# A fused attention and int8 feed-forward kernel: where the sums of the probabilities grow, and how wide they are when the ones product takes them

## The chip, the cores and the metric

The kernel runs on one core of a Trainium2 chip. TensorE (PE) multiplies matrices and writes to PSUM, VectorE (DVE) and ScalarE (ACT) work element by element, GpSimd (POOL) does a little at the ends, and SyncE (SP) issues most transfers. The metric is the device time of one execution in microseconds: 1489.73 us before, the median of three runs (1487.76 to 1489.96). Each engine takes its instructions in the written order; between engines the order comes from waits on semaphores.

## The reference

Cross attention of 1024 queries against 2048 context rows, for 2 batch entries and 16 heads of 64, then a feed-forward product in int8. What matters here is the attention:

```python
q = (lat @ Wq); k, v = split(ctx @ Wkv); k = apply_rope(k, cos, sin)
attn = einsum('bhnd,bhsd->bhns', q, k) * 64 ** -0.5
attn = clip(attn, -11.0, 11.0)
attn = softmax(attn, axis=-1)
out  = einsum('bhns,bhsd->bhnd', attn, v) @ Wo + bo
x    = x + tanh(g_xattn) * out
# then: layer norm, rows scaled to int8, times an int8 matrix, gated and added
```

The softmax needs, for each query and head, the sum of 2048 exponentials. The kernel clips after the exponential (CLIP_LOW is e^-11, CLIP_HIGH is e^11), adds the clipped values on VectorE as far as the rows go on different partitions, and sums over the 128 partitions with a matrix of ones on TensorE.

## The kernel before

It has three stages: projections (up to about 475 us of the span), attention (to about 1369 us), and the output stage. The change lies in attention, `attention` from L760 on, and in `PairEnds`, which turns sums into reciprocals.

Attention goes over 16 *pairs* of heads (n). A pair has 32 *units*: for each of two *halves* of 512 queries, 16 steps of 128 context rows. A unit's scores for both heads are 1024 columns in one of three PSUM banks. Four units are a *batch*, so a pair has 8 batches b, numbered 0 to 7; batches 0 to 3 are the first half and 4 to 7 the second. In all there are 32 halves.

The engines share the work so:
- TensorE, for each batch: the scores of batch b (`scores`, 24 matmuls), then the values of batch b-1 (`values`, the product of probabilities and v, accumulated in `value_ps` over a half). Once per half, in batches 1 and 5, it multiplies the sums with ones into `sum_ps` (`sums`, L914): four products, one for each of two heads and of two sums, each into its own 32 partitions.
- ScalarE: the exponentials of each unit into `prob` (L966). `prob` has two places of 4096 columns, taken in turn. It also copies `value_ps` and `sum_ps` to SBUF once per half (L973, L979).
- VectorE, for each batch: the clip in place, 4096 columns (`clip`, L1050), then the additions (`add_probs`). Batch 0 or 4 adds its two halves of 2048 columns into `prob_sum` (L1062); the other three batches each add their two halves to it, one after the other (L1066). In batches 1 and 5 `normalise` (L206) multiplies the output of the half before by its reciprocal sums; in batches 3 and 7 `reciprocals` adds the two reloaded sums of 8 columns (L192) and inverts them (L197).
- SyncE: the sums to DRAM and back in another layout, reciprocals likewise, output, and the k, q and v of the pair after next.

The order on each engine is written out by hand (the `pair` function of each), for the most part inside a loop that runs over two pairs at a time. What holds the parts together around the change: a clip waits for its four exponentials (`exped`), values wait for the clip (`clipped`), an addition waits for the one before (`added`), ones wait for all additions of the half, and an exponential waits until the place in `prob` that it writes has been multiplied (`valued`) and added.

Of the kernel before, what the change touches and what calls it, by code (L numbers as in the profile page):

```python
# [12 lines left out]
P = 128  # L13
# [26 lines left out]
def flamingo_kernel(  # L40
# [20 lines left out]
    sum_scr = nc.dram_tensor("sum_scr", (ALLPAIRS, 2, 4, CH), F32, kind="Internal").ap()  # L61
# [60 lines left out]
class Late:  # L122

    def __init__(self, sb, sem, o_raw, o_out):
# [10 lines left out]
        self.sum_row = sb("sum_row", [P, CH])  # L135
        self.sum_sq = sb("sum_sq", [P, 2, 4, CH // P])
        self.sum_both = sb("sum_both", [P, 2, 2, CH // P])
# [6 lines left out]
        self.sum_joined = sem("sum_joined")  # L144
# [7 lines left out]
class PairEnds:  # L152
# [9 lines left out]
    def load_sums(self, sp, n, half):  # L162
        late = self.late
        sp.wait_ge(late.sum_stored, 16 * (2 * n + half + 1))
        sp.dma_start(late.sum_sq[:, half, :, :], self.sum_scr[n, half].rearrange("g (p j) -> p g j", p=P)
                     ).then_inc(late.sum_in[half], 16)
# [21 lines left out]
    def reciprocals(self, dve, n, half):  # L188
        late = self.late
        turn = 2 * n + half  # L190
        dve.wait_ge(late.sum_in[half], 16 * (n + 1))
        dve.tensor_tensor(late.sum_both[:, half, :, :], late.sum_sq[:, half, 0:2, :], late.sum_sq[:, half, 2:4, :],  # L192
                          ALU.add).then_inc(late.sum_joined, 1)
        dve.wait_ge(late.sum_joined, turn + 1)
        if not isinstance(n, int) or n >= 1:
            dve.wait_ge(late.rec_stored[half], 16 * n)
        dve.reciprocal(late.rec_sq[:, half, :, :], late.sum_both[:, half, :, :]).then_inc(late.rec_made, 1)  # L197
# [557 lines left out]
def attention(nc, ctx, load_pair, k_st, q_st, v_st, kqv_in, v_stored, late, ends, gate_tanh, wo, bo, rhs_t,  # L755
# [8 lines left out]
    ADDS = 2 * HALF_BATCHES - 1  # L764
# [4 lines left out]
    prob_sum = sb("prob_sum", [P, 2, 2, 2, CH])  # L769
# [33 lines left out]
    def first(n, k=1):  # L803

        return isinstance(n, int) and n < k

# [67 lines left out]
    def _(pe):  # L874
# [17 lines left out]
        def values(n, slot, b):  # L892
# [3 lines left out]
            for i in range(BATCH_UNITS):  # L896
                s = (b * BATCH_UNITS + i) % STEPS
                for a in range(2):
                    rows = slice(a * DHEAD, (a + 1) * DHEAD)
                    last = pe.matmul(value_ps[rows, :], v_st[slot][:, s, rows], prob[:, b % 2, i, a * CH:(a + 1) * CH],  # L900
                                     start=(s == 0), stop=(s == STEPS - 1))
            last.then_inc(valued, 1)

        def sums(n, half):
# [6 lines left out]
            for j in range(2):  # L911
                for a in range(2):
                    row = (2 * j + a) * SUM_ROWS
                    last = pe.matmul(sum_ps[row:row + SUM_ROWS, :], ones[:, 0:SUM_ROWS], prob_sum[:, half, j, a, :],  # L914
                                     start=True, stop=True)
# [42 lines left out]
    def _(act):  # L958
        def exps(n, b):
            for u in range(b * BATCH_UNITS, (b + 1) * BATCH_UNITS):  # L960
                if u % BATCH_UNITS == 0 and not (first(n) and b < 2):

                    act.wait_ge(valued, BATCHES * n + b - 1)
                    act.wait_ge(added, ADDS * (2 * n + (b - 2) // HALF_BATCHES) + 2 * ((b - 2) % HALF_BATCHES) + 1)
                act.wait_ge(scored, UNITS * n + u + 1)
                act.activation(prob[:, b % 2, u % BATCH_UNITS, :], score_ps[:, u % BANKS, :, :], ACT.Exp, scale=SCALE  # L966
# [8 lines left out]
        def copy_sums(n, half):  # L975
# [3 lines left out]
            act.activation(late.sum_row[:, :], sum_ps[:, :], ACT.Copy).then_inc(late.sum_copied, 1)  # L979
# [39 lines left out]
    def _(dve):  # L1019
# [27 lines left out]
        def clip(n, b):  # L1047
            tile = prob[:, b % 2, :, :]
# [3 lines left out]
        def add_probs(n, b):  # L1052

            half, part = divmod(b, HALF_BATCHES)
            total = prob_sum[:, half, :, :, :].rearrange("p j a c -> p j (a c)")
            halves = [prob[:, b % 2, j:j + 2, :] for j in (0, 2)]
            before = ADDS * (2 * n + half) + 2 * part - 1
            dve.wait_ge(clipped, BATCHES * n + b + 1)
            if part == 0:
                if not first(n):  # L1060
                    dve.wait_ge(summed, 2 * (n - 1) + half + 1)
                dve.tensor_tensor(total, halves[0], halves[1], ALU.add).then_inc(added, 1)  # L1062
                return
            for j in range(2):
                dve.wait_ge(added, before + j)
                dve.tensor_tensor(total, total, halves[j], ALU.add).then_inc(added, 1)  # L1066
# [355 lines left out]
```

## Time and profile before

| | |
|---|---|
| device time, median of 3 runs | 1489.73 us |
| device time of the profiled execution | 1489.53 us |
| its span | 1487.7 us |
| TensorE busy, share of the span | 98% |
| VectorE busy, share of the span | 84% |
| ScalarE busy, share of the span | 47% |
| values (L900), 2048 records | 468.6 us |
| scores (L888), 3072 records | 396.7 us |
| exponentials (L966), 512 | 483.1 us |
| additions of 2048 columns (L1066 and L1062), 192 and 32 | 446.3 and 75.8 us |
| clips (L1050), 128 | 292.7 us |
| ones products (L914), 256 records | 34.1 us |

An engine's share is an average over three stages, so it can't be read as the load of attention. A float32 matmul leaves two records. The recorded time of one matmul (0.59 us for 512 columns) includes its way through the array, and neighbours overlap, so what a group costs is read from the start of the group to the start of the next. In the idle column, an arrow names what ended the wait.

### The profile page before, as it was taken

The numbers are of one execution on the slowest core, as the hardware profiler recorded it, in microseconds if no ns is written. First come the engines' busy times: TensorE is split into PE (matmuls) and PEld (weight loads), VectorE is DVE, ScalarE is ACT, GpSimd is POOL, SyncE is SP. The second block draws the span as 40 slices with busy tenths as digits, with TensorE's granted clock in tenths as the row PEclk, the third lists the DMA queues.
The fourth block names the chain that finished last, engine by engine and source line by source line (L and its number), as shares of the span: only waits on it lengthen the run. The fifth ranks groups of instructions, "written<-read, shape, count | busy, mean of one in ns | idle before, by whom it ended". The sixth has DMA issues, their size and how long they took to land. (4 is left out here: it accounts for less than half of the span.)

```text
span 1487.7 us, 22575 instructions
## 1 busy us (share of the span) xinstructions
PE 1458.5 (98%) x8090; PEld 886.2 (60%) x8090; DVE 1246.0 (84%) x1108; ACT 706.5 (47%) x823; POOL 118.7 (8%) x71
## 2 busy tenths in 40 slices
PE   8999999999999899999999999999999999999997
PEld 7888888888887344444444444444444444444774
DVE  6756666667655999999999999999999999997997
ACT  4432222222223556565655656565656556564332
POOL 0500000000000300000000000000000000001775
PEclk9999999999999999999999999999999999999998
DMA  7783655555667623523532532541551551402652
GB/s 269 249 260 135 205 170 170 186 157 165 193 172 253 165 48 96 129 60 98 133 70 81 135 92 58 135 101 48 135 127 27 130 134 37 121 16 72 171 169 85
DMA packets 144496, 195.60 MB, mean 131 GB/s; under 512 B 36160, under 2 KB 85312, under 8 KB 138304
## 3 DMA queue, kind: packets, MB, share of 16 engines
q1 hardware_dynamic: 141296, 189.71, 45.3%
q10 hardware_dynamic: 3152, 5.25, 0.9%
q8 instruction: 30, 0.49, 0.1%
q14 instruction: 18, 0.15, 0.0%
HBM read 114.83 MB, written 80.08 MB: 131 GB/s over the span
## 5 line engine op out<-in xcount | busy, mean ns | idle before, releaser
L966 ACT ACTIVATE prob<-score_ps 128x1024 f32<-128x1024 f32 x512 | 483.1, 1032 | 187.1 <-PE score_ps L888 184.3
L900 PE MATMUL value_ps<-prob,v_st 128*64 128x512 f32 x2048 | 468.6, 599 | 4.9 <-DVE prob L1050 4.9
L1066 DVE TENSOR_TENSOR prob_sum<-prob_sum,prob 128x2048 f32<-128x2048 f32 x192 | 446.3, 2325 | 13.6 <-DVE prob L1050 0.2
L888 PE MATMUL score_ps<-q_st,k_st 64*128 64x512 f32 x3072 | 396.7, 403 | 7.9 <-ACT prob L966 5.8
L888 PEld LDWEIGHTS score_ps<-q_st,k_st 64*128 64x128 f32 x3072 | 272.8, 186 | 177.5 <-issue 103.1
L1050 DVE TENSOR_SCALAR prob<-prob 128x4096 f32<-128x4096 f32 x128 | 292.7, 2287 | 41.0 <-ACT prob L966 38.8
L900 PEld LDWEIGHTS value_ps<-prob,v_st 128*64 128x64 f32 x2048 | 135.8, 137 | 272.9 <-issue 265.0
L644 DVE TENSOR_TENSOR k_cos<-k_raw,rope 128x1024 f32<-128x1024 f32 x32 | 39.2, 1225 | 100.0 <-ACT k_raw L548 100.0
L553 ACT ACTIVATE v_out<-proj_ps 128x1024 f32<-128x1024 f32 x31 | 31.9, 1028 | 136.7 <-PE proj_ps L230 136.7
L548 ACT ACTIVATE k_raw<-proj_ps 128x1024 f32<-128x1024 f32 x31 | 31.9, 1029 | 105.1 <-PE proj_ps L230 105.1
L1062 DVE TENSOR_TENSOR prob_sum<-prob 128x2048 f32<-128x2048 f32 x32 | 75.8, 2368 | 1.8 <-DVE prob L1050 0.2
L1386 POOL MEMSET unround<- 128x1 f32 x1 | 0.1, 98 | 844.1 <-POOLq L116 844.1
L230 PE MATMUL proj_ps<-tok_hi,wkv_hi 128*128 128x512 f32 x248 | 67.0, 392 | 0.0
L230 PE MATMUL proj_ps<-tok_hi,wkv_lo 128*128 128x512 f32 x248 | 66.3, 389 | 0.0
L230 PE MATMUL proj_ps<-wkv_lo,tok_hi 128*128 128x512 f32 x248 | 66.3, 389 | 0.0
L230 PE MATMUL proj_ps<-wkv_hi,tok_hi 128*128 128x512 f32 x248 | 66.3, 389 | 0.0
L230 PE MATMUL proj_ps<-wkv_hi,tok_lo 128*128 128x512 f32 x248 | 66.3, 389 | 0.0
L230 PE MATMUL proj_ps<-tok_lo,wkv_hi 128*128 128x512 f32 x248 | 66.3, 389 | 0.0
L979 ACT ACTIVATE sum_row<-sum_ps 128x512 f32<-128x512 f32 x32 | 19.2, 599 | 93.4 <-PE sum_ps L914 93.4
L230 PEld LDWEIGHTS proj_ps<-tok_hi,wkv_lo 128*128 128x128 f32 x248 | 46.6, 188 | 9.8
L230 PEld LDWEIGHTS proj_ps<-wkv_hi,tok_hi 128*128 128x128 f32 x248 | 46.6, 188 | 9.7
L230 PEld LDWEIGHTS proj_ps<-tok_lo,wkv_hi 128*128 128x128 f32 x248 | 46.6, 188 | 9.7
(123 smaller groups left out, 1333.6 us busy)
## 6 DMA issues: line engine op xcount, KB each, us to landing
k_st<-k_scr SPq DMA_DIRECT2D x128, 256.0 KB, 6.5
k_scr<-k_hi SPq DMA_DIRECT2D x64, 256.0 KB, 2.7
v_scr<-v_out SPq DMA_DIRECT2D x32, 512.0 KB, 3.4
k_scr<-k_lo SPq DMA_DIRECT2D x64, 256.0 KB, 4.0
q_st<-q_scr SPq DMA_DIRECT2D x16, 1024.0 KB, 10.9
v_st<-v_scr SPq DMA_DIRECT2D x16, 1024.0 KB, 13.8
q_scr<-q_hi SPq DMA_DIRECT2D x32, 256.0 KB, 4.3
q_scr<-q_lo SPq DMA_DIRECT2D x32, 256.0 KB, 4.4
```

What stands on the lines that cost most here:

```text
L230: last = pe.matmul(acc, s, m, start=(n == 0), stop=(n == len(terms) - 1))
L548: act.activation(k_raw[:, j % 2, :, :], banks(what, j, order), ACT.Copy).then_inc(k_copied, 1)
L553: act.activation(v_out[:, j, :], banks(what, j, order), ACT.Copy).then_inc(v_copied, 1)
L644: last = dve.tensor_tensor(made[:, :, :], k_raw[:, s, :, :], rope[:, slot, f:f + 1, :].broadcast_to((P, 2, CH)), ALU.mult)
L888: last = pe.matmul(score_ps[:, u % BANKS, a, :], k_st[slot][rows, k_part, s * P:(s + 1) * P], q_st[slot][rows, q_part, cols], start=(t == ...
L900: last = pe.matmul(value_ps[rows, :], v_st[slot][:, s, rows], prob[:, b % 2, i, a * CH:(a + 1) * CH], start=(s == 0), stop=(s == STEPS - 1))
L966: act.activation(prob[:, b % 2, u % BATCH_UNITS, :], score_ps[:, u % BANKS, :, :], ACT.Exp, scale=SCALE).then_inc(exped, 1)
L979: act.activation(late.sum_row[:, :], sum_ps[:, :], ACT.Copy).then_inc(late.sum_copied, 1)
L1050: dve.tensor_scalar(tile, tile, CLIP_LOW, CLIP_HIGH, ALU.max, ALU.min).then_inc(clipped, 1)
L1062: dve.tensor_tensor(total, halves[0], halves[1], ALU.add).then_inc(added, 1)
L1066: dve.tensor_tensor(total, total, halves[j], ALU.add).then_inc(added, 1)
L1386: pool.memset(unround[:, :], -ROUND).then_inc(unround_set, 1)
```

## The change

It does five things.
- The first batch of a half is no longer added. Its exponentials are written straight into `prob_sum`, which is now as wide as a batch (4096 columns, one for each half). It is clipped there, and TensorE takes its values from there (`home`). The other three batches use the two places of `prob`, six batches of a pair in turn (`tenant` works out who had the place before).
- The other three batches are added in one instruction of 4096 columns each. The first of the three writes over batch 0 or 4, and so waits for `valued` of that batch.
- Behind the last addition of the half, two more fold the sum: 4096 columns into 2048, then 2048 into 1024 (one unit's width). There are 5 additions per half in place of 7 (`ADDS`).
- The ones product has four products of 256 columns in place of four of 512; the copy of `sum_ps` and the sums in DRAM are half as large.
- `reciprocals` has no addition any more: one inversion of the reloaded sums.

VectorE at the end of one half and the start of the next, in the loop: the end of batch 3, then batch 4 and the start of batch 5. L1050 is the clip, L192 the joining addition of 8 columns, L197 the reciprocal, L1062 and L1066 the additions of 2048 columns; the rest is waits and register work. Before:

```order
L192 TENSOR_TENSOR sum_both<-sum_sq 128x8 [waits sum_in1]
L194 REGISTER_ALU
L197 RECIPROCAL rec_sq<-sum_both 128x8 [waits rec_stored1,sum_joined]
L1049 REGISTER_ALU
L1050 TENSOR_SCALAR prob<-prob 128x4096 [waits exped]
L1058 REGISTER_ALU
L1062 TENSOR_TENSOR prob_sum<-prob 128x2048 [waits summed,clipped]
L1049 REGISTER_ALU
L1050 TENSOR_SCALAR prob<-prob 128x4096 [waits exped]
L1058 REGISTER_ALU
L1065 ISA [waits clipped]
L1066 TENSOR_TENSOR prob_sum<-prob_sum,prob 128x2048 [waits added]
```

In the code before, an addition of 2048 columns stands between the clip of batch 4 and that of batch 5, and the addition of batch 5 waits for VectorE's own work only. The same place after, from the first fold on; L1081 and L1083 are the folds, L191 the reciprocal, L1064 the clip, L1078 the wide addition:

```order
L1081 TENSOR_TENSOR prob_sum<-prob_sum 128x2048 [waits added]
L1082 REGISTER_ALU
L1083 TENSOR_TENSOR prob_sum<-prob_sum 128x1024 [waits added]
L191 RECIPROCAL rec_sq<-sum_sq 128x8 [waits rec_stored1,sum_in1]
L1063 REGISTER_ALU
L1064 TENSOR_SCALAR prob_sum<-prob_sum 128x4096 [waits exped]
L1063 REGISTER_ALU
L1064 TENSOR_SCALAR prob<-prob 128x4096 [waits exped]
L1073 REGISTER_ALU
L1075 REGISTER_ALU [waits clipped]
L1078 TENSOR_TENSOR prob_sum<-prob_sum,prob 128x4096 [waits valued]
```

The two folds have come ahead of the clip of batch 4 (the one on `prob_sum`), the addition between the two clips is gone, and the addition of batch 5 stands behind a wait on `valued`.

TensorE around the ones product in batch 1 of the second pair (the last two units' scores, the values of batch 0, the ones product, the next scores), before:

```order
L888 MATMUL score_ps<-q_st,k_st 128x512 [waits exped]
L888 MATMUL score_ps<-q_st,k_st 128x512 x5
L900 MATMUL value_ps<-prob,v_st 64x512 [waits o_copied,clipped]
L900 MATMUL value_ps<-prob,v_st 64x512 x7
L914 MATMUL sum_ps<-prob_sum,ones 32x512 [waits sum_copied,added]
L914 MATMUL sum_ps<-prob_sum,ones 32x512 x3
L888 MATMUL score_ps<-q_st,k_st 128x512 [waits exped]
L888 MATMUL score_ps<-q_st,k_st 128x512 x5
```

The ones product (L914) there has 512 columns for each of its four matmuls. And after:

```order
L896 MATMUL score_ps<-q_st,k_st 128x512 [waits exped]
L896 MATMUL score_ps<-q_st,k_st 128x512 x5
L908 MATMUL value_ps<-prob_sum,v_st 64x512 [waits o_copied,clipped]
L908 MATMUL value_ps<-prob_sum,v_st 64x512 x7
L923 MATMUL sum_ps<-prob_sum,ones 32x256 [waits sum_copied,added]
L923 MATMUL sum_ps<-prob_sum,ones 32x256 x3
L896 MATMUL score_ps<-q_st,k_st 128x512 [waits exped]
L896 MATMUL score_ps<-q_st,k_st 128x512 x5
```

The order is the same; the values of the half's first batch now come from `prob_sum`, and the ones product is half as wide.

```diff
--- before.py
+++ after.py
@@ -58,7 +58,7 @@
 
     k_scr = nc.dram_tensor("k_scr", (BATCH, QUADS, 4, P, NS), F32, kind="Internal").ap()
     v_scr = nc.dram_tensor("v_scr", (BATCH * NS, INNER), F32, kind="Internal").ap()
-    sum_scr = nc.dram_tensor("sum_scr", (ALLPAIRS, 2, 4, CH), F32, kind="Internal").ap()
+    sum_scr = nc.dram_tensor("sum_scr", (ALLPAIRS, 2, 4, CH // 2), F32, kind="Internal").ap()
     rec_scr = nc.dram_tensor("rec_scr", (ALLPAIRS, 2, 2, CH), F32, kind="Internal").ap()
 
     o_scr = nc.dram_tensor("o_scr", (BATCH, INNER, NQ), F32, kind="Internal").ap()
@@ -132,16 +132,14 @@
         self.o_raw = o_raw
         self.o_out = o_out
         self.recip = sb("recip", [P, NQ])
-        self.sum_row = sb("sum_row", [P, CH])
-        self.sum_sq = sb("sum_sq", [P, 2, 4, CH // P])
-        self.sum_both = sb("sum_both", [P, 2, 2, CH // P])
+        self.sum_row = sb("sum_row", [P, CH // 2])
+        self.sum_sq = sb("sum_sq", [P, 2, 2, CH // P])
         self.rec_sq = sb("rec_sq", [P, 2, 2, CH // P])
         self.o_loaded = [sem(f"o_loaded{i}") for i in range(2)]
         self.o_hi_made = sem("o_hi_made3")
         self.sum_copied = sem("sum_copied")
         self.sum_stored = sem("sum_stored")
         self.sum_in = [sem(f"sum_in{i}") for i in range(2)]
-        self.sum_joined = sem("sum_joined")
         self.rec_made = sem("rec_made")
         self.rec_stored = [sem(f"rec_stored{i}") for i in range(2)]
         self.rec_in = [sem(f"rec_in{i}") for i in range(2)]
@@ -162,7 +160,7 @@
     def load_sums(self, sp, n, half):
         late = self.late
         sp.wait_ge(late.sum_stored, 16 * (2 * n + half + 1))
-        sp.dma_start(late.sum_sq[:, half, :, :], self.sum_scr[n, half].rearrange("g (p j) -> p g j", p=P)
+        sp.dma_start(late.sum_sq[:, half, :, :], self.sum_scr[n, half].rearrange("(a h) c -> a (h c)", a=2).rearrange("a (p j) -> p a j", p=P)
                      ).then_inc(late.sum_in[half], 16)
 
     def store_reciprocals(self, sp, n, half):
@@ -187,14 +185,10 @@
 
     def reciprocals(self, dve, n, half):
         late = self.late
-        turn = 2 * n + half
         dve.wait_ge(late.sum_in[half], 16 * (n + 1))
-        dve.tensor_tensor(late.sum_both[:, half, :, :], late.sum_sq[:, half, 0:2, :], late.sum_sq[:, half, 2:4, :],
-                          ALU.add).then_inc(late.sum_joined, 1)
-        dve.wait_ge(late.sum_joined, turn + 1)
         if not isinstance(n, int) or n >= 1:
             dve.wait_ge(late.rec_stored[half], 16 * n)
-        dve.reciprocal(late.rec_sq[:, half, :, :], late.sum_both[:, half, :, :]).then_inc(late.rec_made, 1)
+        dve.reciprocal(late.rec_sq[:, half, :, :], late.sum_sq[:, half, :, :]).then_inc(late.rec_made, 1)
 
     def normalise(self, eng, n, half):
         late = self.late
@@ -761,12 +755,12 @@
     BATCHES = UNITS // BATCH_UNITS
     HALF_BATCHES = BATCHES // 2
     BANKS = 3
-    ADDS = 2 * HALF_BATCHES - 1
+    ADDS = HALF_BATCHES + 1
     k_st.append(sb("k_st1", [P, 2, NS], F32R))
     q_st.append(sb("q_st1", [P, 2, NQ], F32R))
     v_st.append(sb("v_st1", [P, STEPS, P]))
     prob = sb("prob", [P, 2, BATCH_UNITS, 2 * CH])
-    prob_sum = sb("prob_sum", [P, 2, 2, 2, CH])
+    prob_sum = sb("prob_sum", [P, 2, BATCH_UNITS, 2 * CH])
     wo_raw = sb("wo_raw", [P, 2, DIM])
 
     rhs_amax = sb("rhs_amax", [P, KT])
@@ -803,6 +797,20 @@
     def first(n, k=1):
 
         return isinstance(n, int) and n < k
+
+    def home(b):
+
+        half, part = divmod(b, HALF_BATCHES)
+        if part == 0:
+            return prob_sum[:, half, :, :]
+        return prob[:, (half * (HALF_BATCHES - 1) + part - 1) % 2, :, :]
+
+    def tenant(b):
+
+        half, part = divmod(b, HALF_BATCHES)
+        seat = half * (HALF_BATCHES - 1) + part - 1 - 2
+        half, part = divmod(seat % (2 * (HALF_BATCHES - 1)), HALF_BATCHES - 1)
+        return (-1 if seat < 0 else 0), half, part + 1
 
     def all_pairs(eng, body):
 
@@ -897,7 +905,7 @@
                 s = (b * BATCH_UNITS + i) % STEPS
                 for a in range(2):
                     rows = slice(a * DHEAD, (a + 1) * DHEAD)
-                    last = pe.matmul(value_ps[rows, :], v_st[slot][:, s, rows], prob[:, b % 2, i, a * CH:(a + 1) * CH],
+                    last = pe.matmul(value_ps[rows, :], v_st[slot][:, s, rows], home(b)[:, i, a * CH:(a + 1) * CH],
                                      start=(s == 0), stop=(s == STEPS - 1))
             last.then_inc(valued, 1)
 
@@ -908,11 +916,12 @@
                 pe.wait_ge(late.sum_copied, 2 * n + half)
             if first(n, 2) and not first(n) and half == 0:
                 pe.wait_ge(row_copied, 1)
-            for j in range(2):
-                for a in range(2):
-                    row = (2 * j + a) * SUM_ROWS
-                    last = pe.matmul(sum_ps[row:row + SUM_ROWS, :], ones[:, 0:SUM_ROWS], prob_sum[:, half, j, a, :],
-                                     start=True, stop=True)
+            for a in range(2):
+                for part in range(2):
+                    row = (2 * a + part) * SUM_ROWS
+                    col = a * CH + part * CH // 2
+                    last = pe.matmul(sum_ps[row:row + SUM_ROWS, 0:CH // 2], ones[:, 0:SUM_ROWS],
+                                     prob_sum[:, half, 0, col:col + CH // 2], start=True, stop=True)
             last.then_inc(summed, 1)
 
         def turn_rhs(part):
@@ -958,12 +967,17 @@
     def _(act):
         def exps(n, b):
             for u in range(b * BATCH_UNITS, (b + 1) * BATCH_UNITS):
-                if u % BATCH_UNITS == 0 and not (first(n) and b < 2):
-
-                    act.wait_ge(valued, BATCHES * n + b - 1)
-                    act.wait_ge(added, ADDS * (2 * n + (b - 2) // HALF_BATCHES) + 2 * ((b - 2) % HALF_BATCHES) + 1)
+                if u % BATCH_UNITS == 0:
+                    if b % HALF_BATCHES == 0:
+                        if not first(n):
+                            act.wait_ge(summed, 2 * n - 1 + b // HALF_BATCHES)
+                    else:
+                        before, half, part = tenant(b)
+                        if not first(n, -before):
+                            act.wait_ge(valued, BATCHES * (n + before) + half * HALF_BATCHES + part + 1)
+                            act.wait_ge(added, ADDS * (2 * (n + before) + half) + part)
                 act.wait_ge(scored, UNITS * n + u + 1)
-                act.activation(prob[:, b % 2, u % BATCH_UNITS, :], score_ps[:, u % BANKS, :, :], ACT.Exp, scale=SCALE
+                act.activation(home(b)[:, u % BATCH_UNITS, :], score_ps[:, u % BANKS, :, :], ACT.Exp, scale=SCALE
                                ).then_inc(exped, 1)
 
         def copy_values(n, half):
@@ -976,7 +990,7 @@
             act.wait_ge(summed, 2 * n + half + 1)
             if not (first(n) and half == 0):
                 act.wait_ge(late.sum_stored, 16 * (2 * n + half))
-            act.activation(late.sum_row[:, :], sum_ps[:, :], ACT.Copy).then_inc(late.sum_copied, 1)
+            act.activation(late.sum_row[:, :], sum_ps[:, 0:CH // 2], ACT.Copy).then_inc(late.sum_copied, 1)
 
         def copy_rhs(part):
             act.wait_ge(rhs_turned, part + 1)
@@ -1045,25 +1059,28 @@
                 made.then_inc(rhs_step, 1)
 
         def clip(n, b):
-            tile = prob[:, b % 2, :, :]
+            tile = home(b)
             dve.wait_ge(exped, UNITS * n + (b + 1) * BATCH_UNITS)
             dve.tensor_scalar(tile, tile, CLIP_LOW, CLIP_HIGH, ALU.max, ALU.min).then_inc(clipped, 1)
 
         def add_probs(n, b):
 
             half, part = divmod(b, HALF_BATCHES)
-            total = prob_sum[:, half, :, :, :].rearrange("p j a c -> p j (a c)")
-            halves = [prob[:, b % 2, j:j + 2, :] for j in (0, 2)]
-            before = ADDS * (2 * n + half) + 2 * part - 1
+            if part == 0:
+                return
+            total = prob_sum[:, half, :, :]
+            before = ADDS * (2 * n + half) + part - 1
             dve.wait_ge(clipped, BATCHES * n + b + 1)
-            if part == 0:
-                if not first(n):
-                    dve.wait_ge(summed, 2 * (n - 1) + half + 1)
-                dve.tensor_tensor(total, halves[0], halves[1], ALU.add).then_inc(added, 1)
-                return
-            for j in range(2):
-                dve.wait_ge(added, before + j)
-                dve.tensor_tensor(total, total, halves[j], ALU.add).then_inc(added, 1)
+            if part == 1:
+                dve.wait_ge(valued, BATCHES * n + b)
+            else:
+                dve.wait_ge(added, before)
+            dve.tensor_tensor(total, total, home(b), ALU.add).then_inc(added, 1)
+            if part == HALF_BATCHES - 1:
+                dve.wait_ge(added, before + 1)
+                dve.tensor_tensor(total[:, 0:2, :], total[:, 0:2, :], total[:, 2:4, :], ALU.add).then_inc(added, 1)
+                dve.wait_ge(added, before + 2)
+                dve.tensor_tensor(total[:, 0, :], total[:, 0, :], total[:, 1, :], ALU.add).then_inc(added, 1)
 
         def pair(n, slot):
             for b in range(BATCHES):
```

## Rows read from the trace of the kernel before

**Rows 1.** the page's first part, busy time of each engine

```profile
PE 1458.5 (98%) x8090; PEld 886.2 (60%) x8090; DVE 1246.0 (84%) x1108; ACT 706.5 (47%) x823; POOL 118.7 (8%) x71
```

**Rows 2.** busy time by stretch: PE, PEld, DVE, ACT, POOL, granted clock, DMA share, GB/s

```profile
500.00:520.00 20.00, 14.99 (x82) 6.77 (x80) 19.80 (x12) 9.93 (x11) 7.27 (x2) 0.91 0.28 88
540.00:560.00 20.00, 17.47 (x106) 7.53 (x104) 19.79 (x15) 10.49 (x12) 0.00 (x0) 1.00 0.51 109
620.00:680.00 60.00, 60.00 (x370) 28.01 (x369) 56.98 (x32) 35.27 (x40) 0.00 (x0) 1.00 0.43 107
```

**Rows 3.** timeline of TensorE, one half: start us, us, instruction

```profile
637.36 1.06 PE L914 MATMUL sum_ps<-prob_sum,ones 128*32 128x512 f32 x8
638.36 3.05 PE L888 MATMUL score_ps<-q_st,k_st 64*128 64x512 f32 x24
641.34 3.65 PE L900 MATMUL value_ps<-prob,v_st 128*64 128x512 f32 x16
...
661.03 3.65 PE L900 MATMUL value_ps<-prob,v_st 128*64 128x512 f32 x16
664.61 1.07 PE L914 MATMUL sum_ps<-prob_sum,ones 128*32 128x512 f32 x8
```

**Rows 4.** timeline of VectorE, the same half

```profile
635.61 2.29 DVE L1050 TENSOR_SCALAR prob<-prob 128x4096 f32<-128x4096 f32 x1 [0.88 <-ACT prob L966]
638.04 4.62 DVE L1066 TENSOR_TENSOR prob_sum<-prob_sum,prob 128x2048 f32<-128x2048 f32 x2
642.58 0.68 DVE L206 TENSOR_TENSOR o_out<-o_raw,recip 128x512 f32<-128x512 f32 x1
643.18 2.29 DVE L1050 TENSOR_SCALAR prob<-prob 128x4096 f32<-128x4096 f32 x1
645.59 4.62 DVE L1066 TENSOR_TENSOR prob_sum<-prob_sum,prob 128x2048 f32<-128x2048 f32 x2
...
657.26 0.20 DVE L197 RECIPROCAL rec_sq<-sum_both 128x8 f32<-128x8 f32 x1
657.38 2.29 DVE L1050 TENSOR_SCALAR prob<-prob 128x4096 f32<-128x4096 f32 x1
659.71 2.29 DVE L1062 TENSOR_TENSOR prob_sum<-prob 128x2048 f32<-128x2048 f32 x1
```

**Rows 5.** VectorE additions: groups by line; one line's min/median/max ns

```profile
L644 DVE TENSOR_TENSOR k_cos<-k_raw,rope 128x1024 f32<-128x1024 f32 x32 | 39.2, 1225 | 100.0 <-ACT k_raw L548 100.0
L1066 DVE TENSOR_TENSOR prob_sum<-prob_sum,prob x192: 2291/2292/4380, 488.0 to 1365.2; 128x2048 f32<-128x2048 f32 x192
```

**Rows 6.** timeline of TensorE in the first two pairs and at the end

```profile
517.50 4.50 PE L900 MATMUL value_ps<-prob,v_st 128*64 128x512 f32 x16
521.94 1.06 PE L914 MATMUL sum_ps<-prob_sum,ones 128*32 128x512 f32 x8
...
549.28 3.66 PE L900 MATMUL value_ps<-prob,v_st 128*64 128x512 f32 x16 [1.40 <-DVE prob L1050]
552.87 1.07 PE L914 MATMUL sum_ps<-prob_sum,ones 128*32 128x512 f32 x8
...
582.65 1.07 PE L914 MATMUL sum_ps<-prob_sum,ones 128*32 128x512 f32 x8
...
1347.81 1.06 PE L914 MATMUL sum_ps<-prob_sum,ones 128*32 128x512 f32 x8
...
1367.55 1.07 PE L914 MATMUL sum_ps<-prob_sum,ones 128*32 128x512 f32 x8 [1.00 <-DVE prob_sum L1066]
```

**Rows 7.** timeline of VectorE in the first pair

```profile
523.26 6.71 DVE L1066 TENSOR_TENSOR prob_sum<-prob_sum,prob 128x2048 f32<-128x2048 f32 x2
...
545.98 1.05 DVE L1044 TENSOR_SCALAR rhs_int<-rhs_raw 128x512 bf16<-128x512 f32 x3
546.94 2.29 DVE L1050 TENSOR_SCALAR prob<-prob 128x4096 f32<-128x4096 f32 x1
```

**Rows 8.** groups by line, VectorE's clip

```profile
L1050 DVE TENSOR_SCALAR prob<-prob 128x4096 f32<-128x4096 f32 x128 | 292.7, 2287 | 41.0 <-ACT prob L966 38.8 <-issue 1.6
```

## The prediction

> **What bounds the kernel now.** I read the page's shares first. TensorE is busy 98% of the span, VectorE 84%, ScalarE 47% [rows 1]. The 84% is an average over stages, so next I read a steady stretch of attention: from 620 to 680 us TensorE is busy 60.00 of 60, at full granted clock, and VectorE 56.98 [rows 2]. VectorE has 5% of slack there, and the change gives it work.
>
> The third view is the timeline of one half: four batches (5, 6, 7 of one pair, then 0 of the next) and the ones product. From one ones product to the next are 27.25 us (637.36 to 664.61) without an idle gap [rows 3]: TensorE sets the pace. Per batch it runs scores (2.98 us) and then the values of the batch *before* (3.58 us), so a batch costs 6.56 us. The ones product adds 1.00 us.
>
> VectorE in the same half [rows 4] has one gap that the data causes: 0.88 us before the clip of batch 5, waiting for ScalarE's exponentials. From that clip to the clip of batch 0 it runs without a break. That clip ends at 659.67, and TensorE wants it at 661.03: 1.4 us of slack. This is the number that the change spends. After the clip of batch 0, VectorE does the half's first addition (2.29 us) while it would wait for the next exponentials anyway, so this addition is free today.
>
> **The change, part by part.** *The free addition goes, and two folds appear.* Batch 0 (and 4) needs no addition. In the half's last batch two folds of 2048 and 1024 columns follow its addition, and the clip of the next batch 0 is queued behind them on VectorE. Work leaves the place where it was hidden and arrives in the place where there were 1.4 us.
>
> *Prices on VectorE.* A 2048-column addition takes 2.292 us, a 1024-column one 1.225 [rows 5]: 1.067 us per 1024 columns. No row has 4096. By the slope it is 2.292 + 2.134 = 4.43 us. The lower end is the slope with no fixed part, 4.27; the upper end is today's pair of additions, 4.62 [rows 4]. I take 4.43. An independent instruction starts 0.08 us before the recorded end of the one ahead (the pair starts at 638.04, lasts 4.62, and the next starts at 642.58), a dependent one 0.04 behind it (4.62 - 2x2.29). So a wide addition holds the engine 4.35 us, or 4.47 if a fold waits for it; the folds 2.33 and 1.23 - 0.08 = 1.15. Per half the additions and folds are 4.35 + 4.35 + 4.47 + 2.33 + 1.15 = 16.65 us, against 3x4.54 + 2.21 = 15.83 today. The joining addition of 8 columns goes, 0.2 us. Net +0.6 us per half: small. What decides is order.
>
> The Trainium skill, "VectorE: DVE Perf Modes", section on the TRN2 errata, holds that the fixed latency is paid once per instruction, so that a single large tile is cheaper, and its rules for kernel authors say to minimise the number of instructions. By that rule alone the change helps: eight instructions become five, about 0.16 us each by the two additions above. The rows agree on the fixed part, but the columns added per half (three times 4096, 2048 and 1024 against seven times 2048) are 1024 more, 1.07 us, so the rule's gain of some 0.5 us is outweighed.
>
> *The new wait.* The addition of batch 1 (5) writes over batch 0 (4), so it waits until TensorE has finished that batch's values. This closes a loop: clip of batch 0, then values of batch 0, then addition of batch 1, then everything of the half on VectorE, then the next clip of batch 0. Queued behind the waiting addition are all later clips, for which TensorE's values wait. VectorE can put only the clip of batch 1 into the 3.65 us of the values.
>
> *The loop, summed,* from the first addition of a half, at A, each from its start to the next start [rows 4]: addition 4.35, normalise 0.60, clip 2.41, addition 4.35, clip 2.41, addition 4.47, folds 2.33 and 1.15, reciprocal 0.12, clip 2.29: 24.48 us. Then values start 0.06 behind the clip (today's stalled example: 546.94 + 2.29 to 549.28 [rows 6, 7]), take 3.65, and the addition starts 0.05 later: 28.24.
> One wait lies inside: the clip of batch 2 (6) needs its exponentials. The ones product starts at A - 0.12, the scores follow, and the clip comes 4.82 us after the scores' start (638.36 to 643.18 [rows 3, 4]).
> The ones product's price: values are eight rounds of two column groups in 3.58 us, today's ones two rounds of four groups in 1.00; so 0.43 per 512-column round and 0.14 fixed. Half the columns give 2x0.215 + 0.14 = 0.57 us (bounds 0.50 and 1.00, the latter if the columns did not count). So that clip starts at A - 0.12 + 0.57 + 4.82 = A + 5.27 and not A + 4.95: +0.32.
> **The loop is 28.56 us.** TensorE needs 27.33 - 0.43 = 26.90, so it idles 1.66 us per half, before the values of batch 0 or 4. The 0.43 us saved on the ones product is lost in that idle time.
>
> *What is hidden.* ScalarE copies 512 columns less 256, and the transfer of sums halves: ScalarE is busy 47% [rows 1], and the copy is on no path but at the very end. SyncE's queue keeps its order; VectorE asks for the reloaded sums behind the folds now, 3.5 us later than before, so what is on time today stays on time. ScalarE's new waits (older values, additions, ones products) are over before scores arrive: batch 7's seat is free when batch 5 is added, A + 4.4, and its scores start at A + 7.0.
>
> **The sum over the run.** The ones products mark the halves [rows 3, 6]: today 521.94, 552.87, 582.65, then 28 steady ones to 1347.81 (27.33 each), and the last at 1367.55.
> - Up to 521.94: VectorE loses the first addition (2.2) and 3x0.2 on the wide ones and gains 3.5 of folds, +0.7; but the values of batch 4 at 517.50 wait there for scores and not for the clip. Between 0 and 0.7, I take 0.
> - 521.94 to 552.87 (30.93): the loop without normalise, with the quantising of the weights between (three gaps, 3.04 us in all; 545.98 to 546.94 is one) and one addition stretched by GpSimd's subtraction (6.71 for 4.62) [rows 7]: 24.48 - 0.60 + 3.04 + 2.09 + 3.76 = 32.77. +1.8.
> - 552.87 to 582.65: TensorE has transposes of its own there and stays the slow one: -0.4.
> - 28 steady halves: 28x28.56 - 765.16 = +34.5. Pauses on issue before VectorE's clips, 1.6 us in all [rows 8] and hidden now, join the loop: +1.5.
> - The end: the last ones product needs both folds. From the one before: 0.12 + 5.27 + 2.41 + 4.35 + 2.41 + 4.47 + 2.33 + 1.23 + 0.05 = 22.64 against 19.74; the product and its copy are some 0.6 shorter before the output stage may start. +2.3.
>
> Sum +39.7 us. The profiled execution took 1489.53 us, so 1529.2. The median of the runs shown is 1489.73, 0.2 above it, so I say 1529.
>
> **The rivals.**
> - *VectorE's throughput alone decides; the loop costs nothing.* It speaks for it that VectorE is the fuller engine after the change. The half would be 24.48 - 0.08 + 2.41 + 0.32 = 27.13 us, 0.20 under today: 1483. It decides from the point at which the values of batch 0 end before the clip of batch 1 does. Against it: values take 3.65 us, the clip 2.41, and both start from the same clip.
> - *TensorE stays the bound* and the saving on the ones shows in full: 32x0.43 = 13.8 us, 1476. That needs the clip of batch 0 to end within 1.4 us of where it ends now, and the folds are 3.5.
> - *The clock falls in the new stalls.* From 500 to 520 us TensorE is busy 14.99 of 20, the granted clock is 0.91 over the stretch (so it fell from the 2.4 GHz level to the 1.2 one for a part of it), and a group of values takes 4.50 and not 3.65 [rows 2, 6]. From 540 to 560 it is busy 17.47 of 20, with one stall of 1.40 us, the clock stays 1.00 and the values take 3.66. The new stall, 1.66 in 28.56, is nearer to the second. A fall in each half adds 0.85 us to the loop: +27, 1556.
> - *The wide addition is not 4.43.* At 4.27 the loop is 0.48 shorter and the time 1514; at 4.62 it is 0.57 longer: 1547.
>
> **How the numbers follow.** The loop with its sum: 0.79, its own range 1520 to 1538. The wide addition near an end: 0.07. A fall of the clock, in all or some halves: 0.07. VectorE's throughput alone: 0.04. TensorE the bound: 0.03. The range takes the addition's two ends, 1514 to 1547, and leaves out the gains and a full fall of the clock. A difference under 0.2% (3 us) can't be told from none. Faster than that: the two gaining cases, 0.07. Within: 0.01, where a case would just cancel. Slower: 0.92.
>
> **What would show it.** In the profile after, ones products 28.5 us apart; TensorE idle some 1.6 us before the values of batch 0 and 4, released by VectorE's clip, and VectorE idle some 1.5 us (3.76 - 2.21) around the clip of batch 1 and 5, the larger part before the addition, released by TensorE's values. A wide addition of 4.43 us, a ones product of 0.57. TensorE's share falls from 98% to about 94 or 95. The forecast is wrong if that stall is missing, if the clip of batch 0 is not behind the folds, or if the ones products stand under 27.3 us apart.

## The result, and the profile after

The changed kernel takes 1531.04 us (median of 5, 1530.15 to 1531.95) against 1489.55 (5 runs, 1487.58 to 1489.96): ratio 1.0281, 95% interval 1.0267 to 1.0295. It is slower by 41.5 us; 1529 was forecast. The span of the profiled execution went from 1487.7 to 1528.1, +40.4 us.

The first part of the page of the changed kernel answers to [rows 1]:

```profile
PE 1450.7 (95%) x8090; PEld 888.3 (58%) x8090; DVE 1261.6 (83%) x1012; ACT 700.2 (46%) x823; POOL 121.5 (8%) x71
```

TensorE works 7.8 us less and VectorE 15.6 us more, in a span that is 40 us longer. Neither amount explains the 40 us, so the engines must wait where they did not before. Here is busy time by stretch of the changed kernel (columns as in [rows 2]):

```profile
545.00:555.00 10.00, 6.15 (x28) 2.03 (x30) 6.86 (x8) 1.32 (x3) 0.00 (x0) 0.83 0.64 136
640.00:700.00 60.00, 56.65 (x362) 27.54 (x362) 55.31 (x23) 33.47 (x39) 0.00 (x0) 1.00 0.36 89
1406.00:1416.00 10.00, 9.26 (x33) 7.29 (x30) 0.78 (x2) 3.64 (x5) 6.03 (x4) 0.70 0.63 183
```

In the steady stretch *no* engine is full: TensorE 56.65 of 60, VectorE 55.31. Before, TensorE was at 60.00. When two engines both wait, look for a loop between them. The timeline of TensorE in the changed kernel, one half, answers to [rows 3]:

```profile
640.36 0.64 PE L923 MATMUL sum_ps<-prob_sum,ones 128*32 128x256 f32 x8
640.93 3.05 PE L896 MATMUL score_ps<-q_st,k_st 64*128 64x512 f32 x24
...
660.62 3.04 PE L896 MATMUL score_ps<-q_st,k_st 64*128 64x512 f32 x24
665.34 3.65 PE L908 MATMUL value_ps<-prob_sum,v_st 128*64 128x512 f32 x16 [1.68 <-DVE prob_sum L1064]
668.92 0.64 PE L923 MATMUL sum_ps<-prob_sum,ones 128*32 128x256 f32 x8
```

The ones products stand 28.56 us apart (668.92 - 640.36), and the only gap is 1.68 us before the values of the half's first batch, ended by VectorE's clip. The ones product itself costs 0.57 (640.36 to 640.93), as worked out. The timeline of VectorE in the same half answers to [rows 4]:

```profile
640.47 4.43 DVE L1078 TENSOR_TENSOR prob_sum<-prob_sum,prob 128x4096 f32<-128x4096 f32 x1 [1.29 <-PE value_ps L908]
644.81 0.69 DVE L200 TENSOR_TENSOR o_out<-o_raw,recip 128x512 f32<-128x512 f32 x1
645.74 2.29 DVE L1064 TENSOR_SCALAR prob<-prob 128x4096 f32<-128x4096 f32 x1 [0.23 <-ACT prob L980]
648.17 4.42 DVE L1078 TENSOR_TENSOR prob_sum<-prob_sum,prob 128x4096 f32<-128x4096 f32 x1
...
659.38 2.29 DVE L1081 TENSOR_TENSOR prob_sum<-prob_sum 128x2048 f32<-128x2048 f32 x1
661.71 1.22 DVE L1083 TENSOR_TENSOR prob_sum<-prob_sum 128x1024 f32<-128x1024 f32 x1
662.85 0.19 DVE L191 RECIPROCAL rec_sq<-sum_sq 128x8 f32<-128x8 f32 x1
662.97 2.24 DVE L1064 TENSOR_SCALAR prob_sum<-prob_sum 128x4096 f32<-128x4096 f32 x1
665.43 2.29 DVE L1064 TENSOR_SCALAR prob<-prob 128x4096 f32<-128x4096 f32 x1 [0.23 <-ACT prob L980]
669.04 4.43 DVE L1078 TENSOR_TENSOR prob_sum<-prob_sum,prob 128x4096 f32<-128x4096 f32 x1 [1.31 <-PE value_ps L908]
```

The folds (659.38, 661.71) stand in front of the clip at 662.97, and the values at 665.34 follow its end (665.21) at once. VectorE then waits 1.31 us for these values. That is 1.54 us around this clip with the 0.23 before it (665.43), where some 1.5 were forecast. The 0.23 us before the clip of batch 2 or 6 (645.74), ended by ScalarE's exponentials, looks harmless; experiment e3 shows that it is as much a part of the loop as the 1.31.

Where the 40.4 us lie, by the starts of the ones products in the two traces: up to the first -2.7 (521.94 to 519.29); first to second +3.7; second to third -0.4; the 28 steady halves +34.2 (799.34 less 765.16, 28.55 us each); the last +2.8; the output stage +2.8.

### The profile page after: what moved, and what is told of

Same layout as the page of the kernel before. It is cut to its first block and busy times, and to the rows that moved or that the text cites. A ratio compares the mean times of both kernels' runs of the same rounds, so it can differ in the third digit from the quotient of the medians.

```text
span 1528.1 us, 22339 instructions
## 1 busy us (share of the span) xinstructions
PE 1450.7 (95%) x8090; PEld 888.3 (58%) x8090; DVE 1261.6 (83%) x1012; ACT 700.2 (46%) x823; POOL 121.5 (8%) x71
## 5 line engine op out<-in xcount | busy, mean ns | idle before, releaser
L1078 DVE TENSOR_TENSOR prob_sum<-prob_sum,prob 128x4096 f32<-128x4096 f32 x96 | 424.8, 4425 | 45.0 <-PE value_ps L908 37.9
L980 ACT ACTIVATE prob<-score_ps 128x1024 f32<-128x1024 f32 x384 | 362.2, 1031 | 109.6 <-PE score_ps L896 108.5
L908 PE MATMUL value_ps<-prob,v_st 128*64 128x512 f32 x1536 | 352.6, 601 | 1.4 <-DVE prob L1064 1.4
L1064 DVE TENSOR_SCALAR prob<-prob 128x4096 f32<-128x4096 f32 x96 | 220.4, 2296 | 20.0 <-ACT prob L980 20.0
L908 PEld LDWEIGHTS value_ps<-prob,v_st 128*64 128x64 f32 x1536 | 102.2, 137 | 203.3 <-issue 200.2
L908 PE MATMUL value_ps<-prob_sum,v_st 128*64 128x512 f32 x512 | 118.4, 605 | 49.3 <-DVE prob_sum L1064 49.3
L980 ACT ACTIVATE prob_sum<-score_ps 128x1024 f32<-128x1024 f32 x128 | 120.8, 1032 | 82.4 <-PE score_ps L896 82.4
L908 PEld LDWEIGHTS value_ps<-prob_sum,v_st 128*64 128x64 f32 x512 | 35.1, 138 | 118.2 <-issue 105.7
L1064 DVE TENSOR_SCALAR prob_sum<-prob_sum 128x4096 f32<-128x4096 f32 x32 | 71.8, 2245 | 10.9 <-ACT prob_sum L980 10.9
L1081 DVE TENSOR_TENSOR prob_sum<-prob_sum 128x2048 f32<-128x2048 f32 x32 | 75.4, 2356 | 1.1
```

The lines of the kernel that those rows point to most:

```text
L980: act.activation(home(b)[:, u % BATCH_UNITS, :], score_ps[:, u % BANKS, :, :], ACT.Exp, scale=SCALE).then_inc(exped, 1)
L1064: dve.tensor_scalar(tile, tile, CLIP_LOW, CLIP_HIGH, ALU.max, ALU.min).then_inc(clipped, 1)
L1078: dve.tensor_tensor(total, total, home(b), ALU.add).then_inc(added, 1)
L1081: dve.tensor_tensor(total[:, 0:2, :], total[:, 0:2, :], total[:, 2:4, :], ALU.add).then_inc(added, 1)
```

## The experiments

Each ran beside the kernel before, on the same chip as it (e1 to e4 on one chip, e5 to e7 on another); ratios are to it. Code cuts are shortened, `...` marks what is left out. Line numbers in the rows are of each kernel's own text.

**e1: the folds behind the next clip.** The additions and folds are those of the changed kernel.

```diff
                 clip(n, b)
+                if b == 0 and not first(n):
+                    fold(n - 1, 1)
+                if b == HALF_BATCHES:
+                    fold(n, 0)
                 add_probs(n, b)
+                if b == BATCHES - 1 and isinstance(n, int) and n == ALLPAIRS - 1:
+                    fold(n, 1)
...
```

`fold(n, half)` holds the same two folds, which are gone from `add_probs`.

> The changed kernel with only the place of the two folds changed: they come behind the clip of the next half's first batch. Nothing else moves, the wait on values stays. Theory A (the folds ahead of that clip hold the values, and so close the loop): VectorE's clip of batch 0 or 4 ends some 3.5 us sooner, TensorE has no stall, and the ones products stand 26.90 us apart (27.33 of before less 0.43 for the narrower ones): about 1478 us, with 2 to 3 us lost at the end of attention. Theory B (the wait on values itself is the cost): VectorE still idles before the first addition and the halves stay near 28.2 us, about 1520. Theory C (VectorE's throughput is the bound after the change): 27.1 us per half, about 1484.

Measured: 1478.12 us (5 runs), ratio 0.993 (0.9917 to 0.9944). The ones products stand 26.90 us apart over 28 steady halves. Timeline of VectorE in e1:

```profile
647.17 4.43 DVE L1078 TENSOR_TENSOR prob_sum<-prob_sum,prob 128x4096 f32<-128x4096 f32 x1
651.52 0.20 DVE L191 RECIPROCAL rec_sq<-sum_sq 128x8 f32<-128x8 f32 x1
651.63 2.24 DVE L1064 TENSOR_SCALAR prob_sum<-prob_sum 128x4096 f32<-128x4096 f32 x1
653.79 2.28 DVE L1084 TENSOR_TENSOR prob_sum<-prob_sum 128x2048 f32<-128x2048 f32 x1
656.11 1.23 DVE L1086 TENSOR_TENSOR prob_sum<-prob_sum 128x1024 f32<-128x1024 f32 x1
657.44 2.29 DVE L1064 TENSOR_SCALAR prob<-prob 128x4096 f32<-128x4096 f32 x1
659.86 4.42 DVE L1078 TENSOR_TENSOR prob_sum<-prob_sum,prob 128x4096 f32<-128x4096 f32 x1
```

The same instructions with the same durations; the folds now fill the place in which VectorE would wait for exponentials, and the addition at 659.86, which still waits for the values by its semaphore, does not wait in fact. TensorE has no stall there: it is busy 270.00 us of the 270 from 906 to 1176 us. Moving two instructions is worth 3.5% by the two ratios, some 52 us. Theory A stands; B (the wait itself costs) falls; C (VectorE's throughput) falls, since 26.90 is TensorE's own time. VectorE, busy 264.18 of the same 270, is close behind it, as e7 shows.

**e2: no folds.**

```diff
-    ADDS = HALF_BATCHES + 1
+    ADDS = HALF_BATCHES - 1
...
-            if part == HALF_BATCHES - 1:
-                dve.wait_ge(added, before + 1)
-                dve.tensor_tensor(total[:, 0:2, :], total[:, 0:2, :], total[:, 2:4, :], ALU.add).then_inc(added, 1)
-                dve.wait_ge(added, before + 2)
-                dve.tensor_tensor(total[:, 0, :], total[:, 0, :], total[:, 1, :], ALU.add).then_inc(added, 1)
```

It leaves out three quarters of each sum: the ones product takes the first unit's columns only.

> The changed kernel without the two folds (it leaves out three of the four units of each batch from the sums; the ones product takes the first unit). Wide additions and the wait on values stay. Theory A: 3.5 us less ahead of the clip of batch 0 or 4, loop 25.1 us, under TensorE's 26.90: TensorE is the bound, about 1474 us, and no stall before values. Theory B: the wait on values costs by itself, over 1500. Against e1 it tells what the folds cost as work rather than by their place: nothing by A (but for 3.5 us at the end).

Measured: 1471.65 us (4 runs), ratio 0.9889 (0.9874 to 0.9904); a steady half takes 26.89 us (1330.16 less 577.20, by 28), as in e1 (26.90). So the folds, 3.5 us of VectorE's time per half, cost nothing as work in the steady halves while they lie behind the clip. The two times are 6.5 us apart. Of the 8.1 us between the two traces (1477.4 and 1469.3), 3.6 lie in the last half and 3.0 behind it (see e5), 1.3 ahead of the first ones product.

**e3: no wait on values.** The first addition of a half writes into a small tile of its own, in four instructions of 1024 columns, so it need not wait for the values; it leaves out this addition's part of the sums.

```diff
...
             if part == 1:
-                dve.wait_ge(valued, BATCHES * n + b)
-            else:
-                dve.wait_ge(added, before)
+                for j in range(4):
+                    if j or half or not first(n):
+                        dve.wait_ge(added, before - 3 + j)
+                    dve.tensor_tensor(aside[:, :], total[:, j, :], home(b)[:, j, :], ALU.add).then_inc(added, 1)
+                return
+            if part == 2:
+                dve.wait_ge(valued, BATCHES * n + b - 1)
+            dve.wait_ge(added, before)
             dve.tensor_tensor(total, total, home(b), ALU.add).then_inc(added, 1)
...
```

> The changed kernel with the first addition of each half written aside, in four instructions of 1024 columns into a small tile, so that it need not wait for the values of the batch it would write over (the sums lack batches 0, 1, 4 and 5's addition: the second addition adds to batch 0 alone). The folds stay where they are. Theory A': the wait on values is only one of two ways in which the loop closes; clip of batch 0, values, ones, scores of batch 2, exponentials, clip of batch 2 is as long (19.53 + 0.06 + 3.58 + 0.57 + 4.82 = 28.56 us), so the halves stay at 28.5 and the time within 5 us of 1531. Theory B (the wait on values closes the loop, and without it VectorE's throughput of 27.1 or TensorE decides): 1483 to 1490 us.

Measured: 1534.56 us (4 runs), ratio 1.031 (1.0294 to 1.0326); 28.62 us per half. Timeline of VectorE in e3:

```profile
640.16 2.29 DVE L1065 TENSOR_SCALAR prob<-prob 128x4096 f32<-128x4096 f32 x1 [0.18 <-ACT prob L981]
642.59 5.00 DVE L1079 TENSOR_TENSOR aside<-prob_sum,prob 128x1024 f32<-128x1024 f32 x4
647.51 0.68 DVE L200 TENSOR_TENSOR o_out<-o_raw,recip 128x512 f32<-128x512 f32 x1
649.08 2.29 DVE L1065 TENSOR_SCALAR prob<-prob 128x4096 f32<-128x4096 f32 x1 [0.89 <-ACT prob L981]
```

The wait before the first addition is gone (642.59 follows the clip directly), and the idle time has moved to the clip of batch 2 or 6: 0.89 us, for exponentials whose scores come after the late values. The four narrow additions take 5.00 us and not 4.43, but they end before those exponentials do, so their extra 0.57 us is not in the loop. The half is as long as in the changed kernel. A' stands: the new wait that one sees in the diff is worth nothing when it is taken away alone.

**e4: the narrower sum alone, in the kernel before.**

```diff
+            if part == HALF_BATCHES - 1:
+                dve.wait_ge(added, before + 2)
+                dve.tensor_tensor(total[:, 0, :], total[:, 0, :], total[:, 1, :], ALU.add).then_inc(added, 1)
```

(The ones product, its copy, the stored sums and the reciprocals as in the changed kernel.)

> The kernel before with only the narrower sum: a third fold of 1024 columns ahead of the clip of batch 0 or 4, the ones product with half the columns, no joining addition; the first batch is still added, in the two places of prob, in additions of 2048 columns. Theory A: the clip of batch 0 or 4 ends 1.1 us later, within the 1.4 us of slack; TensorE saves 0.43 us, but VectorE is then full: 26.37 busy + 1.25 - 0.2 = 27.4 us per half against 27.33: 1489 to 1494 us. Rival (the saved columns of the ones show since TensorE was the bound): 1476 us.

Measured: 1494.0 us (5 runs), ratio 1.0041 (1.0028 to 1.0055). The ones products stand 27.38 us apart (1349.70 less 583.18, by 28), and TensorE waits 0.4 to 0.5 us per half for the clip. So half the columns for the ones, alone, gains nothing in the steady halves: VectorE has no room for the third fold as long as it also adds the first batch. The small loss as a whole is mostly elsewhere. Of the 4.3 us between the traces (1492.0 and 1487.7) the 28 steady halves hold 1.4; the first pair holds 2.9, the last half 1.1 and what follows it 1.3, while the first ones product comes 1.9 sooner and the next half is 0.4 shorter.

**e5: e1 with its end mended.**

```diff
-            for a in range(2):
+            units = BATCH_UNITS if last_half else 1
+            for u in range(units):
+                for a in range(2):
...
-                    last = pe.matmul(sum_ps[row:row + SUM_ROWS, 0:CH // 2], ones[:, 0:SUM_ROWS],
-                                     prob_sum[:, half, 0, col:col + CH // 2], start=True, stop=True)
+                        last = pe.matmul(sum_ps[row:row + SUM_ROWS, 0:CH // 2], ones[:, 0:SUM_ROWS],
+                                         prob_sum[:, half, u, col:col + CH // 2], start=(u == 0), stop=(u == units - 1))
...
```

The last half's two folds are gone as well.

> e1 with the end mended: the last half of the last pair has no folds; its ones product takes the four units one after the other and lets them add up in PSUM (16 matmuls of 256 columns, about 1.0 us, for 3.5 us of folds and 0.57). Theory A: TensorE waits 0.9 us there and not 4.39, the output stage starts 3.1 us sooner, and its first products keep the full clock (3.75 and 3.21 us in e1 against 2.08 and 1.99 in e2, 3 us in all): 1472 us. Rival (the output stage waits for something else at its start, and the slow products come from that): at most 3 us less than e1, 1475 to 1478.

Measured: 1473.41 us (4 runs), ratio 0.9896 (0.988 to 0.9913). TensorE at the end of attention, first in e1:

```profile
1354.30 0.64 PE L923 MATMUL sum_ps<-prob_sum,ones 128*32 128x256 f32 x8 [4.39 <-DVE prob_sum L1086]
1355.70 3.75 PE L1252 MATMUL wo_ps<-wo_hi,o_hi 128*128 128x512 f32 x8 [0.76 <-PEq L116]
1359.25 3.21 PE L1252 MATMUL wo_ps<-wo_lo,o_hi 128*128 128x512 f32 x8
```

and then in e5:

```profile
1350.62 1.93 PE L926 MATMUL sum_ps<-prob_sum,ones 128*32 128x256 f32 x32 [0.81 <-DVE prob_sum L1081]
1353.31 2.08 PE L1253 MATMUL wo_ps<-wo_hi,o_hi 128*128 128x512 f32 x8 [0.76 <-PEq L116]
1355.23 1.99 PE L1253 MATMUL wo_ps<-wo_lo,o_hi 128*128 128x512 f32 x8
```

The idle time fell from 4.39 to 0.81 us, and the first two groups of the output stage take 4.07 us and not 6.96. The expectation miscounted the ones product: its 32 records are eight rounds over four column groups, 8x0.215 + 0.14 = 1.86 us, not the 1.0 of four rounds, and 1.93 was recorded. So the output stage starts 2.4 us sooner and not 3.1. This version is 1.0% faster than the kernel before.

**e6: one fold.**

```diff
-                dve.wait_ge(added, before + 2)
-                dve.tensor_tensor(total[:, 0, :], total[:, 0, :], total[:, 1, :], ALU.add).then_inc(added, 1)
```

(The ones product, its copy, the sums and the joining addition as in the kernel before.)

> The changed kernel without its second fold: the ones product takes two units as before (512 columns, 1.00 us), and the joining addition of 8 columns is back. Folds stay ahead of the clip. Theory A (the loop with its wait for exponentials): 1.15 + 0.04 us less on VectorE, 0.2 more for the joining addition, 0.43 more on TensorE ahead of the scores of batch 2, all within the loop: 28.56 - 1.19 + 0.19 + 0.43 = 28.0 us, about 1513. Rival (only VectorE's chain counts, TensorE's ones are beside it): 28.56 - 1.0 = 27.55, 1500 us.

Measured: 1512.91 us (4 runs), ratio 1.016 (1.0143 to 1.0177); 28.03 us per half (1367.63 less 582.80, by 28). VectorE lost 1.0 us of work ahead of the clip, but the half became only 0.52 us shorter (the rival asked for 1.0): the 0.43 us that the wider ones product costs TensorE are in the loop too. This is the second sign, beside e3, that the loop runs through ones, scores and exponentials.

**e7: e1 with additions of 2048 columns.**

```diff
-            dve.tensor_tensor(total, total, home(b), ALU.add).then_inc(added, 1)
+            for j in range(2):
+                if j:
+                    dve.wait_ge(added, before + 1)
+                units = slice(2 * j, 2 * j + 2)
+                dve.tensor_tensor(total[:, units, :], total[:, units, :], home(b)[:, units, :], ALU.add).then_inc(added, 1)
```

> e1 with each addition of 4096 columns in two of 2048, as before (six of them per half, 4.54 us a pair for 4.35). Theory A: VectorE's own chain per half goes from 26.7 to 27.3 us, over TensorE's 26.90, so the halves stand 27.28 us apart: 1489 us. Rival (the width is of no account, TensorE's 26.90 stays the bound): 1478 us.

Measured: 1486.31 us (10 runs, 1485.58 to 1491.44), ratio 0.9985 (0.9975 to 0.9995); 27.11 us per half (1341.08 less 582.06, by 28). The width does count once VectorE is nearly full, by 0.21 us per half on the mean of 28 where 0.38 was expected. The mean hides two regimes. The first five of the 28 halves take 26.8 to 27.0 us, as in e1, and TensorE still has no stall before the values. Then VectorE's delay has added up to the point at which TensorE waits for its clip in each half:

```profile
930.10 3.65 PE L908 MATMUL value_ps<-prob_sum,v_st 128*64 128x512 f32 x16 [0.22 <-DVE prob_sum L1064]
```

From 743 to 1233 us the halves are 27.17 us long, VectorE's own chain without a gap, against 26.86 in the same stretch of e1: 0.31 us, near the 0.38 of theory A, whose sum had the chain at 27.28. Of the 10.6 us between the traces of e1 and e7 (1477.4 and 1488.0) the 28 halves hold 5.8; the first pair holds 3.3 (32.74 us for 29.40) and the last half 1.3.

## Why the prediction was right

- *Loop of 28.56 us.* Measured 28.55. Its terms: wide addition 4.43 (4.425 on the mean of 96), folds 2.29 and 1.22, stall 1.68 for 1.66 forecast, ones product 0.57. So the price without a row, taken by the slope of [rows 5], was right.
- *Order decides, not work.* e1 and e2 show it: with the same work in another place the loss turns into the gain that TensorE's saving allows.
- *The cause of the loop was told half right.* The text called the wait on `valued` the thing that closes the loop, and entered the wait for exponentials as a term inside it. e3 shows that the second path (clip of the first batch, values, ones, scores, exponentials, clip of the third batch) is as long by itself (28.62 us without the wait on values; by the prediction's own terms 28.56 against 28.24 through that wait), so the wait on values costs nothing of its own. The sum was right because it took the later of the two at that place. What makes both loops long is the same: the folds ahead of the clip.
- *Fewer, larger instructions.* The Trainium skill, "VectorE: DVE Perf Modes", Rules for kernel authors, says to minimise the number of operations. e7 agrees that this has a value here, 0.31 us per half, once VectorE sets the pace; in the changed kernel it was outweighed as the prediction had it.
- *Luck in the total.* The forecast sum, 39.7 us, is 0.7 off the 40.4 between the traces, but its parts are further off and cancel: up to the first ones product -2.7 against 0, the first pair +3.7 against +1.8, the steady halves +34.2 against +36.0, the end +5.6 against +2.3. The loop is confirmed by the steady halves (34.5 from the loop alone), not by how close the total came.
- *Sizes that were off.* Pauses on issue were to add 1.5 us to the loop; 34.2 was measured for the steady halves where 36.0 was forecast, so they didn't. The first half gained 2.7 us where 0 was taken: the first ones product came at 519.29. Why is open; e4, with the additions of the kernel before, has it early too (520.01). Between the first two ones products 34.65 us passed, not 32.77; 1.5 of these 1.9 us are slow values (next point). At the end the wait for both folds was right (22.51 us for 22.64), but what follows took 2.8 us more than before, where 0.6 less was taken.
- *The clock.* The rival was wrong for the steady halves: over 60 us with two stalls of 1.68 the granted clock is 1.00. But it holds at two places. In the first pair VectorE's quantising adds to the folds, TensorE idles 4.61 us, and the values take 5.16 us, not 3.65; the granted clock of 545 to 555 us is 0.83. At the end of attention it idles 4.39 us, and its first groups take 3.75 and 2.78 us against 2.09 and 1.98, with 0.70 granted from 1406 to 1416 us. That is some 4 us of the 40, not in the forecast sum. (From 500 to 520 us it is low in both kernels, 0.83 granted now and 0.91 before.) The lines:

```profile
548.85 5.16 PE L908 MATMUL value_ps<-prob_sum,v_st 128*64 128x512 f32 x16 [4.61 <-DVE prob_sum L1064]
1406.89 3.75 PE L1243 MATMUL wo_ps<-wo_hi,o_hi 128*128 128x512 f32 x8 [0.74 <-PEq L116]
1410.43 2.78 PE L1243 MATMUL wo_ps<-wo_lo,o_hi 128*128 128x512 f32 x8
```

## What to carry to other kernels

Before adding work to an engine, find in its timeline the one instruction that another engine waits for, and count the slack ahead of it; work put in front of it costs, the same work behind it can be free. When neither engine is full after a change, sum the loop between them, and take at each joint the later of all its waits: removing the one that the trace names may only uncover another of the same length. A saving on the bounding engine is worth its full amount only if that engine keeps its work without a stall.

## What the runs showed of the hardware that had not been expected

A rather short pause is followed by a low clock at the end of attention. Before the output stage TensorE waits twice, for the last ones product and then 0.74 to 0.97 us for the stage's start. The last pause and what follows, in e4:

```profile
1370.51 0.64 PE L909 MATMUL sum_ps<-prob_sum,ones 128*32 128x256 f32 x8 [2.26 <-DVE prob_sum L1064]
1371.90 3.58 PE L1224 MATMUL wo_ps<-wo_hi,o_hi 128*128 128x512 f32 x8 [0.76 <-PEq L116]
1375.28 2.10 PE L1224 MATMUL wo_ps<-wo_lo,o_hi 128*128 128x512 f32 x8
```

With a first wait of 0.81 us (e2, e5) or 1.00 (before) the first group of the stage (eight records) takes 2.08 or 2.09 us, the full clock of 2.4 GHz (1.00 granted from 1353 to 1357 us in e5). With 2.26 (e4) it takes 3.58, with 3.13 (e6) 3.46, with 4.39 (the changed kernel, e1, e3) 3.75: near the 1.2 GHz level for most of the group. The granted clock is 0.64 from 1371 to 1375 us in e4, and 0.50, the 1.2 GHz level throughout, from 1391 to 1395 us in e6. So a wait of 2.3 us there costs 1.5 us more than itself, while the stalls of 1.68 us in the steady halves, each alone in 28.56 us of work, cost nothing more. Whether it is the 0.6 us of length or the second pause close behind that makes the difference, no run here separates.
